# Causal mask by float32 products, one DMA per fixed-row fill, and GpSimd's first block in another order

## What is computed

```python
x = x + L0_xattn(layernorm(x), ctx)          # A0
x = x + L0_ffn(layernorm(x))                 # F0, weights and activations rounded to a grid
x = x + L1_xattn(layernorm(x), ctx)          # A1
x = x + L1_ffn(layernorm(x))                 # F1, 8 experts, top 2, one shared
x = x + L2_xattn(layernorm(x), ctx, mask)    # A2, a full 256x512 mask
x = x + L2_block(layernorm(x))               # AS and F2, below
x = x + L3_xattn(ctx, layernorm(x), mask)    # A3
x = x + L3_ffn(layernorm(x))                 # F3

# AS: causal self-attention over 256 tokens
scores = einsum('bqhd,bkhd->bhqk', q, k)
scores = where(arange(t)[:, None] < arange(t)[None, :], -inf, scores)
attn = softmax(scores / sqrt(8))
```

## Time and profile before

| | |
|---|---|
| median of 3 runs | 2042.76 us (2041.43 to 2043.42) |
| the profiled execution | 2041.18 us |
| its span, first to last instruction | 2039.4 us |
| mean granted clock of PE | 0.896 |
| PE busy | 1857.1 us (91%) |
| DVE busy | 1151.3 us (56%) |
| ACT busy | 1096.2 us (54%) |
| POOL busy | 590.7 us (29%) |
| chain that ended last, by engine | PE 77%, DVE 8%, issue 7%, ACT 4% |

### The profile page before, as it was taken

How to read it: one execution, slowest core, us unless ns; L and a number is a source line. 1 busy time by engine, 2 the same in 40 slices (tenths; PEclk the granted TensorE clock), 3 DMA queues, 4 the chain that set the end, 5 groups by cost and what they waited for, 6 DMA issues and landing times.

```text
span 2039.4 us, 38938 instructions
## 1 busy us (share of the span) xinstructions
PE 1857.1 (91%) x14476; PEld 1195.3 (59%) x14476; DVE 1151.3 (56%) x3394; ACT 1096.2 (54%) x2172; POOL 590.7 (29%) x1171
## 2 busy tenths in 40 slices
PE   3999965899979999899999999997997999989997
PEld 1455534455559988634444555556885455569997
DVE  4788845688842233267777533334664788834342
ACT  0788840588854444256666533333331788854443
POOL 4344312233221222123333422212333444212221
PEclk9999987799989999889999855557997899989999
DMA  4433200445300000132322322100002454100000
GB/s 121 130 120 120 72 16 25 130 150 170 97 7 1 1 1 1 59 114 81 115 69 68 99 82 64 55 25 1 1 1 69 140 160 148 57 1 6 6 6 6
DMA packets 114882, 132.38 MB, mean 65 GB/s; under 512 B 14962, under 2 KB 78728, under 8 KB 114696
## 3 DMA queue, kind: packets, MB, share of 16 engines
q1 hardware_dynamic: 114696, 129.90, 21.1%
HBM read 83.45 MB, written 46.40 MB: 64 GB/s over the span
## 4 chain that ended last, share of the span: by engine, by line
PE 77%; DVE 8%; issue 7%; ACT 4%; POOL 1%; DMA 1%; SPq 0%; POOLq 0%; DVEq 0%
PE ps_av L1086 13%; PE ps_s L1311 13%; PE ps_s L1042 13%; PE ps_t L1289 9%; PE ps_t L1058 5%; DVE mx L1443 4%; PE ps_s L1289 3%; PE ps_t L1071 3%; PE ps_m L1142 2%; PE ps_m L1094 2%; PE ps_m L1128 2%; ACT prob L851 2%; PE ps_m L1134 2%; PE ps_t L1062 2%; PE ps_m L1121 2%
## 5 line engine op out<-in xcount | busy, mean ns | idle before, releaser
L851 ACT ACTIVATE prob<-ps_t 128x512 f32<-128x512 f32 (+1 forms) x1152 | 628.9, 583 | 229.5 <-PE ps_t L1058 145.6
L1443 DVE TENSOR_REDUCE mx<-ps_s 128x1 f32<-128x512 f32 x768 | 491.2, 683 | 117.5 <-PE ps_s L1042 110.3
L1042 PE MATMUL ps_s<-kst,qst 32*128 32x512 f32 (+2 forms) x1280 | 380.8, 514 | 42.2 <-DVE mx L1443 26.7
L1086 PE MATMUL ps_av<-prob,vaug 128*32 128x256 f32 (+1 forms) x4608 | 379.3, 405 | 3.2 <-ACT avs L892 3.2
L1058 PE MATMUL ps_t<-qmx,kst 32*128 32x256 f32 (+1 forms) x2304 | 339.4, 347 | 0.1
L1042 PEld LDWEIGHTS ps_s<-kst,qst 32*128 32x128 f32 x1280 | 159.3, 204 | 274.6 <-issue 151.1
L1311 PEld LDWEIGHTS ps_s<-w_ffn,prob 128*128 128x128 f32 x2688 | 314.1, 192 | 8.3
L1311 PE MATMUL ps_s<-w_ffn,prob 128*128 128x128 f32 x2688 | 318.4, 275 | 0.0
L991 ACT ACTIVATE prob<-ps_t,b1c 128x512 f32<-128x512 f32 x204 | 125.3, 685 | 240.1 <-PE ps_t L1289 240.1
L1677 DVE SCALAR_TENSOR_TENSOR avs<-ps_s,comb,avs 128x128 f32<-128x128 f32 x336 | 94.6, 344 | 260.4 <-PE ps_s L1311 260.4
L788 POOL TENSOR_TENSOR kst<-w_ffn,kst 128x512 fp32r<-128x512 f32 x100 | 127.1, 1273 | 370.5 <-ACT kst L976 370.5
(11 more groups left out here) (209 smaller groups left out, 2202.1 us busy)
## 6 DMA issues: line engine op xcount, KB each, us to landing
kst<-k_parts SPq DMA_DIRECT2D x128, 256.0 KB, 3.5
qst<-q_parts SPq DMA_DIRECT2D x160, 128.0 KB, 3.8
k_parts<-k_hi SPq DMA_DIRECT2D x64, 256.0 KB, 3.0
q_parts<-q_hi SPq DMA_DIRECT2D x80, 128.0 KB, 2.4
ctxT<-in_ctxT SPq DMA_DIRECT2D x32, 256.0 KB, 2.7
k_parts<-k_lo SPq DMA_DIRECT2D x32, 256.0 KB, 3.2
q_parts<-q_lo SPq DMA_DIRECT2D x40, 128.0 KB, 2.4
w_ffn<-in_F_w SPq DMA_DIRECT2D x18, 256.0 KB, 6.6
```

Of the source, the lines that this page charges most:

```text
L851: nc.scalar.activation(row[:, S * kt:S * kt + w], ps_t[TURN[unit(ph, g, n) % 8]][:, 0:w], ACT.Exp).then_inc(sig["exp_done"], 1)
L1042: pe.matmul(dst, qst[p][strip, g, q * 128:(q + 1) * 128], kst[p][strip, g, 0:nk], start=True, stop=True).then_inc(sig["s_ready"], 1)
L1086: mm = pe.matmul(ps_av[32 * j:32 * j + 32, q0:S], vaug[p][:, kt, HG * g + j, :], prob[:, buf, j, S * kt:S * (kt + 1) - q0], start=(kt == 0 ...
L1443: dve.tensor_reduce(mx[:, buf, i:i + 1], src, AX.X, ALU.max, negate=True).then_inc(sig["max_done"], 1)
```

## The change

Three edits. The triangle of AS is held once, 128x128 in float32, and added with the float32 identity in place of the bf16 one. The fixed rows of a strip become its first eight (row 0 mask, 1 to 3 maximum, 4 mask, 5 to 7 zero) and the parts move to rows 8 to 31, so that one DMA of 16 heads x 8 rows fills each of q and k; the SBUF source has 128 rows, one per head and row. POOL normalises and splits batch 0 right after the first power, then zeroes vaug, normalises batch 1 and takes the other powers. Line numbers in the changed kernel are smaller by one in PE's program.

```diff
-K_ROWS = (1, 1 + 2 * DH, 1 + DH)
-Q_ROWS = (1, 1 + DH, 1 + 2 * DH)
-MAX_ROW = 1 + 3 * DH
+FIXED = 8
+K_ROWS = (FIXED, FIXED + 2 * DH, FIXED + DH)
+Q_ROWS = (FIXED, FIXED + DH, FIXED + 2 * DH)
+MAX_ROW = 1
...
-        caus_T = sb("caus_T", [128, 2, S], BF16)
+        caus_T = sb("caus_T", [128, 128])
...
-                for n, fill, w in (("q", rows_q, S), ("k", rows_k, SK)):
-                    rest = scratch[n][p].rearrange("(h r) w -> r h w", h=H)
-                    for r0, r1 in ((0, 1), (MAX_ROW, STRIP)):
-                        sp.dma_start(rest[r0:r1], fill[r0:r1, :].rearrange("r (o w) -> r o w", o=1).to_broadcast([r1 - r0, H, w]))\
-                          .then_inc(strips_filled[p], 16)
+                for n, fill in (("q", rows_q), ("k", rows_k)):
+                    sp.dma_start(scratch[n][p].rearrange("(h r) w -> h r w", h=H)[:, 0:FIXED, :], fill).then_inc(strips_filled[p], 16)
...
-                            sp.wait_ge(strips_filled[p], 16 * 4)
+                            sp.wait_ge(strips_filled[p], 16 * 2)
...
-                pool.memset(fixed[:, 0, r:r + STRIP * (HG - 1) + 1:STRIP], 1.0)
-            link(pool.memset(fixed[:, 1, :].rearrange("p (j r) -> p j r", j=HG)[:, :, MAX_ROW:MAX_ROW + 3], 1.0))
+                pool.memset(fixed[:, 0, r:r + FIXED * (H - 1) + 1:FIXED], 1.0)
+            link(pool.memset(fixed[:, 1, :].rearrange("p (h r) -> p h r", h=H)[:, :, MAX_ROW:MAX_ROW + 3], 1.0))
...
-            link(pool.memset(caus_T[:, :, :], 0.0))
+            link(pool.memset(caus_T[:, :], 0.0))
...
-            link(pool.affine_select(out=caus_T[:, :, :], in_=caus_T[:, :, :], compare_op=ALU.is_ge, fill=MASKED, base=0, pattern=[[-128, 2], [1, S]], channel_multiplier=-1))
+            link(pool.affine_select(out=caus_T[:, :], in_=caus_T[:, :], compare_op=ALU.is_ge, fill=MASKED, base=0, pattern=[[1, 128]], channel_multiplier=-1))
...
                     split_q(ph, b0)
+                    if ph == "A0":
+                        set_values(0)
                     normalise_batch(ph, b1)
                     if ph == "A0":
+                        for blk in range(1, NBLK):
+                            first_power(blk)
                         set_values(1)
...
             first_power(0)
-            set_values(0)
-            for blk in range(1, NBLK):
-                first_power(blk)
...
-                    mm = pe.matmul(bank[:, :].rearrange("p (c s) -> p c s", c=2)[:, :, 0:128], ident_b[:, :],
-                                   caus_T[:, 0:1, 0:128].to_broadcast([128, 2, 128]), start=False, stop=True)
+                    mm = pe.matmul(bank[:, :].rearrange("p (c s) -> p c s", c=2)[:, :, 0:128], ident[:, :],
+                                   caus_T[:, :].rearrange("p (o q) -> p o q", o=1).to_broadcast([128, 2, 128]), start=False, stop=True)
```

## The result

The changed kernel takes 2016.01 us (median of 3 runs, 2015.5 to 2016.99) against 2042.76 before: ratio 0.987, interval 0.985 to 0.989, 26.8 us less. That lies in the range, but the forecast was 1990, so the kernel gained half of what was promised. The profiled execution took 2015.5 us with a span of 2013.7, and its mean granted clock is 0.939 (0.939 and 0.938 in the other two).

What follows compares the result with a forecast made beforehand. PE was taken to bound AS, at half its clock. 2041.2 - 14 (start) - 79 (clock) + 41 (masks) = 1989, predicted as 1990 for the median; the forecast's own range was 1978 to 2012, the overall range 1976 to 2034.

Steps and rivals of the forecast that it cites:

- What bounds AS: Causal stage AS: PE bounds it, at half its clock for 220.0 us; batch steps 21.8 us at full clock, 34.0 low.
- The 79 us for a whole stretch: AS: gain if the 220.0 us at 0.50 run at full clock, by the factor 0.641; uncertain, 75 to 82.
- Therefore I take it that the clock stays up through AS: AS: float32 masks add 5.1 us of dense full-array products per batch, so the clock holds at 1.00; gain 79 us.
- likeness to A2: A2 is just as full (49.4 of 50 us) and keeps 1.00; AS with float32 masks would resemble it.
- rival (b): AS: the clock falls for part of the stage and comes back, 17.8 us per low body, 2007 to 2042; chance 0.18.
- Rival (a): AS: the clock falls as now and never comes back; masks cost 78 us, total 2105, slower; chance 0.14.
- The price of a float32 mask: AS: 0.53 us per mask at full clock, 0.32 more than bf16; 128 masks cost 41 us, at most 52.
- Theory A: AS: full-array products streaming long enough per mask keep PE at 2.4 GHz; float32 only nearly, because it streams with gaps.
- The start: Start: POOL's xn of batch 0 no longer waits for three powers; gain 14 us, between 6 and 15.
- DVE's weight work: Start: DVE's quantisation of the F0 weights begins at 22.0 instead of 36.55, once all four powers are done.
- first maximum: Start: DVE's first maximum comes near 29 us (wanted at 29.3) in place of 43.81.
- By itself that is worth nothing: Single-DMA fills: x and context come a few us sooner, but nobody waits for the fills, so no gain alone.

Runs made afterwards that it cites:

- experiment 3: Changed kernel with the mask added four times by full-array bf16 products in place of one float32 product: 1988.8 us, ratio 0.974.
- experiment 1: Changed kernel with the mask product in bf16 again, so only the new start remains: 2029.5 us, ratio 0.993.
- experiment 7: Changed kernel with four bf16 products per mask, three of them on only the 32 rows of the head's strip: 2103.4 us, ratio 1.029.
- experiment 2: Kernel before with the 128x128 float32 mask product alone: 2030.4 us, ratio 0.994.
- experiment 8: Changed kernel with the float32 mask product done twice: 2050.6 us, ratio 1.003.
- experiment 10: Kernel before with POOL's new order alone, keeping the old fills and mask: 2041.1 us, ratio 0.998.

## Why the forecast was half right

**What bounds AS: right.** PE bounds it at either clock, and the step per body told the price of the clock. The 79 us for a whole stretch stand: from the first turn of values to the last, experiment 3 has 200.4 us and experiment 1 has 244.2, and experiment 3 pays 4.7 us more per body for its masks (26.5 against 21.8). That makes 43.8 + 8 x 4.7 = 81 us for the clock.

**"Therefore I take it that the clock stays up through AS": the step that failed.** The reasoning behind it (full-array work is what the stage lacked) fits what 3 and 7 show, but whether the float32 form adds enough of it was judged by likeness to A2 and not weighed. It adds nearly enough. The clock held for 107 us, then fell, and it was rival (b), at 0.18, that came: one low stretch, 37.5 us long, that cost 15.5 us, where a whole body at the low clock would have cost some 18. Rival (a), that it never comes back, is what one and two bf16 products and fp32r show, so it was a near thing. That the change came out faster at all is due to the start as much as to the mask: 14 us by experiment 1 and 13 by experiment 2.

**The price of a float32 mask: mis-sized.** The forecast took 0.53 us from L1128, and the mask takes 0.62. The neighbour L1121, a float32 product of the same shape, takes a step of 0.63 us in the trace of before (1150.29 to 1150.92) and would have given the larger value; I had taken one row where two stood:

```profile
1150.29 0.70 PE L1121 MATMUL ps_m<-xnT,w_A 128*128 128x256 f32 x2 [0.15 <-ACT qmx L896]
1150.92 0.42 PE L1086 MATMUL ps_av<-prob,vaug 128*32 128x128 f32 x8
```

The dear part is the first record of a mask. In experiment 8, whose masks have four records, they begin at 1171.89, 1172.21 and 1172.42: 0.32 us to the second, 0.21 from there to the third. The load of weights for L1128 begins 0.12 us ahead of its product, under the bf16 mask; that of the float32 mask begins at 1151.80, its product at 1151.81. So a load that the narrow product ahead doesn't hide would explain the 0.11 us; no experiment isolates it. In experiment 8 the four records take 1.06 us (1173.20 to 1174.26), so that the second product costs only 0.44. The extra per body is 6.1 us, not 5.1, which is 8 us over the stage.

```profile
1173.20 1.13 PE L1062 MATMUL ps_t<-caus_T,ident 128*128 128x256 f32 x4
1174.26 0.64 PE L1086 MATMUL ps_av<-prob,vaug 128*32 128x256 f32 x8
```

**Why float32 is the weaker filler: open.** Theory A has it stream with gaps, but the gap found is too small for that. Against one bf16 product (21.8 us), one float32 product lengthens a body by 6.1 us, of which the 0.11 us at the start of 16 masks are 1.8, so 4.3 are left; the clock falls all the same. Three bf16 products lengthen it by 3.0 us, to 24.8, and in the trace the clock holds. So time filled is not the whole measure: by these traces float32 work counts for less than bf16 work of the same duration, or something else differs that no experiment here isolates.

**The start: right in its mechanism and nearly in its size.** DVE's weight work was forecast at 22.0 and came at 21.98, behind the powers as said. The first maximum came at 30.02, not 29.3, since a small operation on DVE (L1472) took 0.96 us beside POOL's memset, where it had taken 0.17; it ended at 23.66 and the memset at 23.63. Of the 13.8 us, 13.2 are left at A0's first turn of values (82.95 against 96.2) and 12.4 at the end of A2. The rest is lost between; I have not followed where.

**"By itself that is worth nothing": wrong.** I had said that nobody waits for the fills. But x is issued behind them, and in POOL's old order xn of batch 0 waits for x. The same paragraph forecast x sooner by a few microseconds and didn't draw the conclusion; alone the fills give 5.6 us at the first maximum. The sum didn't suffer, since the order takes that wait away. The lower bound for late fills (gain 6) was met nearly exactly by experiment 10 (6.5).

**Gaps or kind of work.** By the Trainium skill ("TensorE: Matmul & The Clock Gate", Why this matters for your kernels) idle gaps are what brings the clock down, and the section names nothing else. Experiments 3 and 7 show that this is not all: with PE busy for 97% of the time in both, one holds 2.4 GHz and the other drops to 1.2. A sentence of the same page sets PE's transposes apart from matmuls in what counts as busy (Part 4: PE-mode transpose); no run here isolates transposes, but experiment 7 shows by its 32-row products that kinds of work can count differently.

## What to carry to other kernels

Where PE is busy and the granted clock is low, look at which part of the array the products fill: a stage of 32-row products stayed at 1.2 GHz here with PE busy for 98% of it, and redundant full-array products paid for themselves: three more bf16 masks cost 4.7 us per body and brought the time from 2029.5 to 1988.8 us. There has to be enough of such filler; too little of it is paid for at the low clock and makes the kernel slower, so try several amounts and look at the clock of each. And when a DMA is made shorter, ask what is issued behind it, not only who waits for it.

## What the runs showed that I had not expected

- Four bf16 products of 128x256 with the same weights take 0.54 us, one float32 product of that shape 0.62 us in the same place.
- Rows count for the clock: three products of 32 rows more per mask, as long as full ones, left the clock to fall 22.7 us after the first turn of values; three full ones kept it up for the whole stage.
- A version beats both kernels: bf16 products repeated, with the new start. Four per mask give 1987 to 1989.5 us, three and four in turn 1980 to 1986, against 2016 for the change. Three alone reach 1976, but not in each run.
- The clock falls at the same place in the traces of the changed kernel and of experiment 2: 107.3 us after the first turn of values, although the whole stage stood 12 us later in the second.
